# Cross attention 0 of a Perceiver-like network on Trainium2: the maximum over two PSUM banks in one VectorE operation

## The reference, cut to what matters

```python
def _mha_cross(x, mem, in_w, in_b, out_w, out_b):
    ...
    q = _split_heads(x @ wq.T + bq, H)
    k = _split_heads(mem @ wk.T + bk, H)
    v = _split_heads(mem @ wv.T + bv, H)
    scores = jnp.einsum('bhqd,bhkd->bhqk', q, k) * (1.0 / math.sqrt(hd))
    attn = jax.nn.softmax(scores, axis=-1)
    out = _merge_heads(jnp.einsum('bhqk,bhkd->bhqd', attn, v))
    return out @ out_w.T + out_b
```

## Time and profile before

| | us |
|---|---|
| median of 3 runs | 3657.43 |
| lowest and highest | 3654.14, 3657.65 |
| the profiled execution | 3659.62 |
| its span on the core | 3656.9 |
| cross attention 0 in it, from the first L977 to the last reduction of the stage | 227.4 to 1125 |
| TensorE busy, share of the span | 3368.5, 92% |
| VectorE busy, share of the span | 2508.6, 69% |
| ScalarE busy, share of the span | 1895.5, 52% |
| all reductions at L1092 (896 of them) | 529.1 |

### The profile page before, as it was taken

The page is one execution under the profiler, slowest core; times in us unless marked ns, Lnnn a source line. Parts: engine busy times, 40 slices in busy tenths (PEclk is TensorE's granted clock), DMA queues, the critical chain, the costliest instruction groups (busy, mean ns, idle before and its releaser), DMA issues. The chain is left out here.

```text
span 3656.9 us, 83216 instructions
## 1 busy us (share of the span) xinstructions
PE 3368.5 (92%) x32913; PEld 2372.4 (65%) x32913; DVE 2508.6 (69%) x7162; ACT 1895.5 (52%) x2944; POOL 1145.4 (31%) x807
## 2 busy tenths in 40 slices
PE   6879999999997787999999999999999998957998
PEld 4646666666665665777777777777777776634555
DVE  5657777778785444777777777777777776675333
ACT  4336666666664222666666666666666664522332
POOL 1043333333331003433444334443344431233000
PEclk9969999999999688999999999999999999978999
DMA  1023333333330011111111111111111101000000
GB/s 52 2 68 75 81 71 76 76 78 73 75 65 1 2 47 41 42 33 35 37 42 42 33 36 37 42 42 33 30 42 42 42 22 47 1 27 1 1 1 12
DMA packets 95125, 146.43 MB, mean 40 GB/s; under 512 B 14961, under 2 KB 72337, under 8 KB 93969
## 3 DMA queue, kind: packets, MB, share of 16 engines
q1 hardware_dynamic: 94736, 141.12, 14.4%
HBM read 100.66 MB, written 1.05 MB: 28 GB/s over the span
## 5 line engine op out<-in xcount | busy, mean ns | idle before, releaser
L2137 DVE SCALAR_TENSOR_TENSOR arena<-banks,arena 128x512 f16<-128x512 f32 (+1 forms) x1024 | 554.4, 583 | 309.2 <-ACT arena L2226 307.9
L2226 ACT ACTIVATE arena<-banks 128x512 f16<-128x512 f32 (+1 forms) x1024 | 471.4, 512 | 399.5 <-PE banks L2044 396.4
L1092 DVE TENSOR_REDUCE arena<-banks 128x1 f32<-128x512 f32 (+1 forms) x896 | 529.1, 627 | 187.1 <-PE banks L977 181.8
L1189 ACT ACTIVATE arena<-banks 128x1024 f32<-128x1024 f32 (+1 forms) x448 | 425.0, 964 | 315.1 <-PE banks L998 312.2
L2149 DVE CUSTOM_DVE_ANT_0 arena<-banks,arena 128x1024 f32<-128x1024 f32 (+1 forms) x512 | 494.3, 987 | 31.0 <-issue 30.7
L2233 ACT ACTIVATE arena<-arena 128x1601 f32<-128x1601 f32 x256 | 417.7, 1632 | 107.3 <-DVE arena L2155 105.3
L2044 PE MATMUL banks<-consts,arena 128*128 128x128 f32 (+1 forms) x3328 | 457.6, 276 | 7.4 <-DVE arena L2137 6.6
L2058 PE MATMUL banks<-arena 128*128 128x256 f16 (+1 forms) x1664 | 456.2, 274 | 0.7 <-ACT arena L2240 0.7
L2060 PE MATMUL banks<-arena 128*128 128x256 f16 (+1 forms) x1664 | 451.3, 271 | 0.0
L2059 PE MATMUL banks<-arena 128*128 128x256 f16 (+1 forms) x1664 | 450.2, 271 | 0.0
L2044 PEld LDWEIGHTS banks<-consts,arena 128*128 128x128 f32 (+1 forms) x3328 | 365.6, 141 | 17.6 <-issue 10.5
(11 more groups left out here) (364 smaller groups left out, 6144.6 us busy)
## 6 DMA issues: line engine op xcount, KB each, us to landing
arena<-in_ctxT SPq DMA_DIRECT2D x64, 800.5 KB, 4.5
arena<-arena SPq DMA_DIRECT2D x768, 50.0 KB, 2.2
arena<-in_ctx SPq DMA_DIRECT2D x32, 768.0 KB
arena<-in_mask SPq DMA_DIRECT2D x32, 200.1 KB, 4.5
arena<-in_m2w SPq DMA_DIRECT2D x3, 2048.0 KB, 8.4
arena<-in_xw SPq DMA_DIRECT2D x1, 2048.0 KB, 11.6
weights<-in_weights SPq DMA_DIRECT2D x1, 1920.0 KB, 7.7
arena<-in_ctx SPq DMA_DIRECT2D x32, 32.5 KB
```

The lines of the kernel that those rows point to most:

```text
L1092: eng.tensor_reduce(o, s, AX, ALU.max).then_inc(a_max, 1)
L1189: eng.activation(pr[0:w, at % 4, :].rearrange("p (x n) -> p x n", x=2)[:, :, 0:n], c.ps[0:w, bank:bank + 2, 0:n], ACT.Exp, scale=scale).th ...
L2137: eng.scalar_tensor_tensor(out=part(ptl, g, gr), in0=turned(gr), scalar=TOP, in1=part(pth, g, gr), op0=ALU.mult, op1=ALU.subtract).then_in ...
L2226: eng.activation(part(pth, g, gr), turned(gr), ACT.Copy, scale=TOP).then_inc(t_high, 1)
```

## The change

The reduction at L1092 took one bank; now one operation takes both banks (1024 columns, or 260 in step 6) and writes both columns of `mxp`. TensorE waits once for a step, ahead of both halves, and counts up `a_ps` once, after the second half. `a_max` and `a_ps` now count 7 a unit. No step is moved.

```diff
@@ pe
+            wait_if(eng, a_max, n * STEPS + a)
             for rt in range(2):
-                wait_if(eng, a_max, n * 14 + 2 * a + rt - 1)
...
-                mm.then_inc(a_ps, 1)
+            mm.then_inc(a_ps, 1)
@@ dve
         def maxima(i, v, a):
             n = unit_no(i, v)
-            for rt in range(2):
-                eng.wait_ge(a_ps, n * 14 + 2 * a + rt + 1)
-                if a < 6:
-                    o = mxp[:, v % 2, a // 3, rt, a % 3:a % 3 + 1]
-                    s = c.ps[:, rt, :]
-                else:
-                    o = mxp[:, v % 2, :, rt, 3]
-                    s = c.ps[:, rt, 0:2 * KL].rearrange("p (s n) -> p s n", n=KL)
-                eng.tensor_reduce(o, s, AX, ALU.max).then_inc(a_max, 1)
+            eng.wait_ge(a_ps, n * STEPS + a + 1)
+            if a < 6:
+                o = mxp[:, v % 2, a // 3, :, a % 3]
+                src = c.ps[:, 0:2, :]
+            else:
+                o = mxp[:, v % 2, :, :, 3].rearrange("p s r -> p r s")
+                src = c.ps[:, 0:2, 0:2 * KL].rearrange("p r (s n) -> p r s n", n=KL)
+            eng.tensor_reduce(o, src, AX, ALU.max).then_inc(a_max, 1)
 
         def spread_max(i, v):
             n = unit_no(i, v)
-            eng.wait_ge(a_max, n * 14 + 14)
+            eng.wait_ge(a_max, n * STEPS + STEPS)
```

## The result

The changed kernel takes 3676.5 us (median of 4 runs, 3673.41 to 3676.91) against 3656.6 for the kernel before in the same comparison: a ratio of 1.0057, with a 95% interval of 1.0042 to 1.0072. It is slower by 20 us, as forecast. That the forecast (3676.4) was met to 0.1 is luck: the terms of the sum were not all right, and their errors cancelled.

What follows compares the result with a forecast made beforehand. TensorE's in-order queue was taken to set the pace, VectorE mattering only at unit ends. Unit ends 13.3, prologue 3.1 and last pair 2.4, say 19 us, on the 3657.4 median gave 3676.4 us, range 3663 to 3690.

Steps and rivals of the forecast that it cites:

- The prices: Double reduction on VectorE: 1.22 us for 1024 columns against 1.29 for two of 512; 0.43 for 260 columns.
- Step 6: Unit end: four short matmuls start together, take 0.31, and the small reduction ends later; loss 0.14 us, or 0.07 if quicker.
- Even end: End of an even unit: TensorE waits for both banks ahead of maxima step 2, so L931 moves by 0.32 us.
- The wait ahead of step 2: New TensorE wait of 0.4 to 0.5 us ahead of maxima step 2 in even units, none in odd ones.
- Odd end: End of an odd unit: the queries projection's loads cover the wait for maxima step 2, so only 0.11 us is lost.
- The sum of the ends: Two units lose 0.43 us; over 62 unit ends, 31 x 0.43 = 13.3 us.
- a rival at 5%: Clock: more TensorE idling lowers the stage's granted clock from 1.00 to 0.97, some 3% of 900 us: 3700; 5%.
- Prologue: First maxima steps, back to back at clock 0.50: 1.92 us a step, 3.1 us lost, between 1.5 and 5.
- last pair: Last two units, without projections: a step takes 1.75 us for 1.37; eight steps, partly covered, lose 2.4 us.
- VectorE's saving: Rival: at unit ends the cheaper reductions shorten VectorE's chain by 0.33 x 62 = 20 us, thus 3637; 6%.
- The fixed cost paid once: Rule weighed: one large tile pays the per-instruction fixed cost once, many small ones each time; alone it favours a faster kernel.
- The delays: Rival: small delays of 0.08 to 0.14 us vanish in existing waits for ScalarE; some +6, 3663; 10%.

Runs made afterwards that it cites:

- e2: Kernel before with double reduction and single hand-over in maxima steps 2, 3 and 4 alone, the others bank by bank: 3658.6 us, ratio 1.0011.
- r3: Kernel before with one move, a unit's last mix put ahead of the next maxima (step 1): 3632.9 us, ratio 0.9933.
- e1: Changed kernel with its single hand-over kept, but two reductions in place of the double one: 3701.9 us, ratio 1.0129 to the kernel before.
- e9: Changed kernel with units 0, 1, 62 and 63 bank by bank as before: 3665.2 us, ratio 1.0040 to the kernel before.
- e4: Changed kernel with steps 5 and 6 bank by bank again, steps 0 to 4 double: 3658.3 us, ratio 1.0010 to the kernel before.

## Why the prediction was right, point by point

**What bounds the kernel.** Right: TensorE's in-order queue, and VectorE only at the ends of units. e2 shows the middle to be free of cost and gain, r3 shows the ends to be TensorE idle time that other work can fill.

**The prices.** Right: 1.223 and 0.430 for 1.22 and 0.43. e1 shows that they are a gain.

**Step 6 (forecast 0.14 a unit).** The mechanism was right (0.35 of new VectorE idle time in every unit), the size was not. Step 5's reduction to the start of the joining took 2.03 for 1.94, so 0.09. The mis-sized term is the four short matmuls: 0.31 was assumed, and all four took 0.24, exactly as long as two. The bound of 0.07 that the text gave for this case was nearly the answer.

**Even end (0.32): 0.23.** Of the missing 0.09, some 0.05 comes from step 6 and 0.04 from the hand-over: from the load to the reduction it took 0.43 to 0.44 where 0.47 was used (627.34 to 627.77). The wait ahead of step 2 came, 0.37 long for 0.4 to 0.5.

**Odd end (0.11): -0.03.** Here a term was missing: 0.07 comes from the cast and its neighbour beside GpSimd, which no step of the sum had looked at. Another 0.05 comes from step 6. The remaining 0.02 is not traced.

**The sum of the ends (13.3): 29 x 0.20 + 4.6.** The typical periods made up 6 of it. Another 4.6 came from three more periods at the lower clock, which the prediction had as a rival at 5%, with a price of 3% of the stage. It was neither absent nor that large. So the total was hit by luck: the ends were sized 7.5 too high, and 4.6 of clock and 1.4 outside the stage filled most of that. The difference of the medians, 19.9, is another 2.5 above that of the two profiled spans. Of the 17.4 between the spans the mechanism as written explains 5.8 + 3.4 + 2.2 = 11.4.

**Prologue (3.1): 3.4; last pair (2.4): 2.2.** Right, by their terms. In the prologue of the changed kernel, still at 0.50:

```profile
229.40 0.10 PEld L977 LDWEIGHTS banks<-arena 64*128 64x128 bf16 x2 [1.83 <-DVE arena L1091]
...
239.06 0.14 PEld L981 LDWEIGHTS banks<-arena 64*128 64x128 bf16 x4 [1.83 <-DVE arena L1091]
...
246.19 0.11 PEld L977 LDWEIGHTS banks<-arena 64*128 64x128 bf16 x2 [0.73 <-DVE arena L1091]
```

Five steps take 239.06 - 229.40 = 9.66, or 1.93 each, forecast 1.92; step 6 stands at 239.06 for 238.92. In the last pair:

```profile
1125.12 0.10 PEld L977 LDWEIGHTS banks<-arena 64*128 64x128 bf16 x2 [0.59 <-DVE arena L1091]
...
1126.83 0.10 PEld L977 LDWEIGHTS banks<-arena 64*128 64x128 bf16 x2 [0.59 <-DVE arena L1091]
```

A step takes 1.71 for the 1.75 forecast. In the trace of e9, which takes the double operation out of both, they are 5.7 shorter together.

**The rivals and the rule.** VectorE's saving does not reach TensorE: it is spent inside the hand-over (e1). The fixed cost paid once, from the Trainium skill's "VectorE: DVE Perf Modes", is stated there of operations that read SBUF; for these reads of PSUM it came to 0.07 a pair. The delays were not absorbed by waits for ScalarE. The operation was one operation of 1.22. Splitting again at the place of the bubble, steps 5 and 6, got 0.27 for two units back (e4): by the rule of the Trainium skill's "Perfetto Trace Analysis" weighed in the prediction, the runs agree.

## What to carry to other kernels

Before two operations on two buffers are merged, look at what the other engine does between them: with only two banks, the gap between the first and the second reduction was the time in which TensorE refilled the first. The merged operation saved 0.07 and its single hand-over cost more, but only where neither engine had other work for that time, namely at the ends of units, in the prologue and in the last pair; in the middle it cost nothing. Where an in-order queue waits, look for a step behind the wait that is ready already: moving one mix ahead of it was worth 23 us, more than the merge could lose or win.

## What the runs showed of the hardware that was not expected

- Four 64-row matmuls of 65 columns, two on each row half, took 0.24 from the first load to the last end, as long as two on one half.
- A VectorE cast of 128x4 from f32 to bf16 took 0.177 alone and 0.317 when it started 0.01 to 0.02 behind a GpSimd operation on SBUF: it ended 0.03 behind that operation's end, 30 times out of 30. The subtraction of 128x4 behind it took 0.170 beside a GpSimd operation that started after it, and 0.24 behind one that had started before it. So it is the order of the two starts that counts, not the overlap, and a shift of 0.1 changes which small operation is held. The Trainium skill, "Perfetto Trace Analysis", Optimizing Scalar/DVE Operations, says that the two engines share an SBUF read port; these rows agree with that, though no run here tells the port from another cause.
- Idle time on TensorE has a second price beside its own length, or comes along with one: 1, 4 and 12 periods at a lower granted clock in the kernel before, the changed kernel and e1, each costing some 1.5. All falls began just behind the end of a unit. e9, with the same periods as the changed kernel and no fall, is the exception that keeps the cause open.
